# Attention over 128 graphs: the score matmuls on 32x64 tiles of the array, from keys stored once and without zero blocks

## What is computed

```python
q, k, v = heads(x @ Wq + bq), heads(x @ Wk + bk), heads(x @ Wv + bv)
scores = jnp.einsum('bhqd,bhkd->bhqk', q, k) * scale
scores = jnp.where(adj[:, None] == 0, -jnp.inf, scores)
attn = softmax(scores)
out = jnp.einsum('bhqk,bhkd->bhqd', attn, v) @ Wo + bo
return layernorm(x + out)
```

## Time and profile before

| | us |
|---|---|
| median of 3 runs | 854.3 |
| lowest, highest | 853.88, 855.64 |
| the profiled execution | 854.11 |
| its span in the trace | 852.3 |

### The profile page before, as it was taken

One profiled execution on the slowest core, in us unless ns is written; L12 is line 12 of the kernel. 1 busy time (PEld: TensorE's weight loads), 2 busy tenths in 40 slices (PEclk: granted clock), 3 DMA queues, 4 the chain that ended last, 5 costly groups with the idle time before them and its releaser, 6 DMA issues.

```text
span 852.3 us, 17597 instructions
## 1 busy us (share of the span) xinstructions
PE 834.7 (98%) x7177; PEld 688.5 (81%) x7177; DVE 540.2 (63%) x726; ACT 284.6 (33%) x401; POOL 479.7 (56%) x412
## 2 busy tenths in 40 slices
PE   8999999999999999999999999999999999999985
PEld 6878888888888888888888888888888878888863
DVE  4675557765567665567665577655577655676685
ACT  6552333332333332343332333423333423423210
POOL 3284567545566554666645575555665545654365
PEclk9999999999999999999999999999999999999998
DMA  8224343133433325333143431334333243321332
GB/s 326 70 81 138 100 142 101 53 116 100 155 99 87 103 67 155 100 109 108 64 132 100 149 97 48 129 88 155 100 88 105 72 147 100 106 76 50 112 97 90
DMA packets 50143, 91.86 MB, mean 108 GB/s; under 512 B 11280, under 2 KB 13328, under 8 KB 47888
## 3 DMA queue, kind: packets, MB, share of 16 engines
q1 hardware_dynamic: 37200, 72.91, 27.1%
q10 hardware_dynamic: 12864, 17.84, 7.5%
HBM read 40.37 MB, written 16.78 MB: 67 GB/s over the span
## 4 chain that ended last, share of the span: by engine, by line
PE 91%; DVE 4%; POOL 2%; issue 1%; ACT 1%; ACTq 1%; DMA 0%; POOLq 0%; DVEq 0%
PE ring L272 20%; PE ring L273 20%; PE ring L274 20%; PE psum_s L323 6%; PE ring L337 6%; PE ring L349 6%; PE ring L350 6%; PE ring L353 6%; ACTq L502 1%; DVE soft L599 1%; POOL qt L184 0%; POOL row L184 0%; DMA qt<-in_wq 0%; DVE top L607 0%; DVE total L611 0%
## 5 line engine op out<-in xcount | busy, mean ns | idle before, releaser
L633 DVE TENSOR_TENSOR row<-ring,row 128x512 f32<-128x512 f32 x60 | 41.5, 691 | 212.4 <-PE ring L353 212.4
L748 POOL TENSOR_TENSOR soft<-soft,top 128x1024 f32<-128x1024 f32 x62 | 118.9, 1918 | 79.6 <-DVE top L607 79.6
L177 POOL TENSOR_TENSOR soft<-soft,inverse 128x1024 f32<-128x1024 f32 x62 | 123.3, 1989 | 25.1 <-DVE inverse L614 22.1
L753 POOL TENSOR_TENSOR shifted<-moments,eps 128x1 f32<-128x1 f32 x64 | 12.1, 189 | 207.4 <-DVE moments L638 207.4
L482 ACT ACTIVATE kt<-ring,bk_slot,in_slot 128x512 f32<-128x512 f32 x128 | 92.5, 773 | 57.0 <-PE ring L274 57.0
L272 PE MATMUL ring<-wv_hi,x_hi 128*128 128x512 f32 x256 | 103.0, 402 | 0.0
L272 PE MATMUL ring<-x_hi,wq_hi 128*128 128x512 f32 x256 | 100.4, 392 | 1.1 <-DVE x_lo L649 1.1
L272 PE MATMUL ring<-x_hi,wk_hi 128*128 128x512 f32 x256 | 99.8, 390 | 0.8 <-ACT kt L482 0.8
L273 PE MATMUL ring<-x_lo,wq_hi 128*128 128x512 f32 x256 | 100.3, 392 | 0.0
L274 PE MATMUL ring<-x_hi,wq_lo 128*128 128x512 f32 x256 | 100.2, 391 | 0.0
L744 POOL TENSOR_TENSOR row<-row,bo 128x512 f32<-128x512 f32 x60 | 78.3, 1305 | 38.6 <-DMA row<-in_x 38.6
(11 more groups left out here) (77 smaller groups left out, 1485.8 us busy)
## 6 DMA issues: line engine op xcount, KB each, us to landing
pt<-soft SPq DMA_DIRECT2D x248, 64.0 KB, 2.3
pt<-soft ACTq DMA_DIRECT2D x248, 64.0 KB, 2.3
x_raw<-in_xt SPq DMA_DIRECT2D x15, 1024.0 KB, 6.5
row<-in_x SPq DMA_DIRECT2D x60, 256.0 KB, 3.2
out_rows<-row SPq DMA_DIRECT2D x60, 256.0 KB, 2.1
adj<-in_adj SPq DMA_DIRECT2D x16, 128.0 KB, 2.6
kt<-in_wk SPq DMA_DIRECT2D x4, 256.0 KB, 7.3
row<-in_wv SPq DMA_DIRECT2D x1, 1024.0 KB, 9.9
```

What stands on the lines that cost most here:

```text
L177: ops.tensor_tensor(soft_of(c), soft_of(c), on_keys(inverse[:, c % 2, :]), ALU.mult).then_inc(done, 1)
L748: nc.gpsimd.tensor_tensor(soft_of(c), soft_of(c), on_keys(top[:, c % 2, :]), ALU.subtract).then_inc(centred, 1)
```

## The change

The keys are stored once (`kt` as large as `qt`), by one ScalarE instruction with the plain bias; `in_slot` and `bk_slot` and what makes them are gone. A score matmul takes one head: 32 rows, 64 columns of weights, 64 moving columns, on a 32x64 tile of the array, of which there are eight. There are 32 for a tile of nodes instead of 16. The four row groups of the array must write to different banks, so `psum_s` is laid out by the head's place in its chunk (`HC`, four banks), and each bank now holds both tiles of a pass. For that reason `mask` waits for the scores of both tiles, `score` for the masks of both tiles of the pass before, and near the end `mix(T - 4)` for the mask of the last tile. The scores come to `soft` in another order of heads; `mix` picks them by it, with the same tiles and columns as before. The mask that GpSimd writes is repeated for the four chunks (1024 elements for each partition instead of 256).

```diff
-        kt = sb("kt", [P, 2, KC, 2 * GT, 2, NODES])
+        kt = sb("kt", [P, 2, KC, D])
...
-        bias = sb("bias", [P, 2, GT, NODES])
+        bias = sb("bias", [P, 2, GT, 2, KC, SQ])
...
-        psum_s = ctx.enter_context(nc.psum_tensor("psum_s", [P, 2, 2, D], F32))
+        psum_s = ctx.enter_context(nc.psum_tensor("psum_s", [P, HC, 2, 2, KC, SQ], F32))
...
             def score(c):
                 buf, t = c // GT % 2, c % GT
-                wait_for(pe, masked, c - 1)
+                wait_for(pe, masked, c // 2 * 2)
...
                     for graph in range(2):
-                        rows = slice(t * P + graph * NODES, t * P + (graph + 1) * NODES)
-                        for pair in range(2):
-
-                            f = slice(pair * 2 * DH, (pair + 1) * 2 * DH)
-                            last = nc.tensor.matmul(
-                                psum_s[graph * NODES:(graph + 1) * NODES, c % 2, pair,
-                                       kc * 2 * NODES:(kc + 1) * 2 * NODES],
-                                qt[f, buf, kc, rows],
-                                kt[f, buf, kc, 2 * t + graph, :, :].rearrange("p s k -> p (s k)"),
-                                start=True, stop=True)
+                        own, rows = (slice(graph * NODES, (graph + 1) * NODES),
+                                     slice(t * P + graph * NODES, t * P + (graph + 1) * NODES))
+                        for r in range(HC):
+                            f = slice(r * DH, (r + 1) * DH)
+                            last = nc.tensor.matmul(psum_s[own, r, c % 2, :, kc, :], qt[f, buf, kc, rows],
+                                                    kt[f, buf, kc, rows].rearrange("p (b k) -> p b k", k=SQ),
+                                                    start=True, stop=True)
...
-                                            pt[:, c % 2, :, r // 2 * 2 * KC + kc * 2 + r % 2, :],
+                                            pt[:, c % 2, :, r * KC + kc, :],
...
-            pe.wait_ge(masked, T - 1)
+            pe.wait_ge(masked, T)
             mix(T - 4)
-            pe.wait_ge(masked, T)
             mix(T - 3)
...
-                for s in range(2):
-                    last = nc.scalar.activation(kt[:, buf, m, :, s, :], by_graph(k_bank(J)), ACT.Identity,
-                                                bias=bk_slot[:, s, m:m + 1], scale=in_slot[:, s:s + 1])
-                last.then_inc(k_done, 1)
+                nc.scalar.activation(kt[:, buf, m, :], k_bank(J), ACT.Identity,
+                                     bias=bk[:, m:m + 1], scale=1.0).then_inc(k_done, 1)
...
-                dve.wait_ge(scored, c + 1)
+                dve.wait_ge(scored, c // 2 * 2 + 2)
...
                 nc.vector.tensor_tensor(
-                    soft_of(c),
-                    psum_s[:, c % 2].rearrange("p r (h b k) -> p (r h) b k", b=2, k=SQ)
-                    .rearrange("p h b k -> p b h k"),
-                    bias[:, c // GT % 2, c % GT, :].rearrange("p (b k) -> p b k", k=SQ).unsqueeze(2)
-                    .to_broadcast([P, 2, HEADS, SQ]),
+                    soft_of(c).rearrange("p b (r c) k -> p b r (c k)", r=HC),
+                    psum_s[:, :, c % 2].rearrange("p r b c k -> p b r (c k)"),
+                    bias[:, c // GT % 2, c % GT].rearrange("p b c k -> p b (c k)").unsqueeze(2)
+                    .to_broadcast([P, 2, HC, KC * SQ]),
                     ALU.add).then_inc(masked, 1)
...
-                nc.gpsimd.tensor_scalar(bias[:, G % 2], adj[:, :, :], 0.0, MASKED, ALU.is_equal,
-                                        ALU.mult).then_inc(bias_done, 1)
+                nc.gpsimd.tensor_scalar(
+                    bias[:, G % 2].rearrange("p t b c k -> p (t b) c k"),
+                    adj[:, :, :].rearrange("p t (b k) -> p (t b) k", k=SQ).unsqueeze(2)
+                    .to_broadcast([P, 2 * GT, KC, SQ]),
+                    0.0, MASKED, ALU.is_equal, ALU.mult).then_inc(bias_done, 1)
```

More of the change, by code:

```diff
@@ L64, in attention_kernel @@
         adj = sb("adj", [P, GT, NODES], I32)
-        bias = sb("bias", [P, 2, GT, NODES])
-        in_slot = sb("in_slot", [P, 2])
-        bk_slot = sb("bk_slot", [P, 2, KC])
+        bias = sb("bias", [P, 2, GT, 2, KC, SQ])
         bq = sb("bq", [P, KC])
@@ L96, in attention_kernel @@
         const_done, warm_done = sem("const_done"), sem("warm_done")
-        slots_done, bk_done, bias_done = sem("slots_done"), sem("bk_done"), sem("bias_done")
+        bias_done = sem("bias_done")
         x_hi_done, x_lo_done = sem("x_hi_done"), sem("x_lo_done")
@@ L110, in attention_kernel @@
         pe_went_on, dve_went_on, pool_went_on = sem("pe_went_on"), sem("dve_went_on"), sem("pool_went_on")
-        w_raw = [qt[:, 1],
-                 kt[:, 1].rearrange("p c g s k -> p (c g s k)")[:, 0:KC * D].rearrange("p (c n) -> p c n", n=D),
-                 row[:, :, :],
+        w_raw = [qt[:, 1], kt[:, 1], row[:, :, :],
                  soft[:, :, :, :, :].rearrange("p a b h k -> p (a b h k)").rearrange("p (c n) -> p c n", n=D)]
@@ L120, in at, with s_bank @@
             return ring[(p % 2 * 2 + n) % 4][:, :]
+        def s_bank(n):
+            return psum_s[:, n].rearrange("p t b c k -> p (t b c k)")
         def v_bank(c):
@@ L138, in ot_bank @@
             if 2 * FULL <= c < 2 * FULL + 2:
-                return psum_s[:, c % 2, 0, :]
+                return s_bank(c % 2 * 2)
             if c >= 2 * FULL + 2:
@@ L148, in y_bank @@
                 return ring[c % 2][:, :]
-            return psum_s[:, c % 2, 1 if c < 2 * FULL + 2 else 0, :]
+            return s_bank(c % 2 * 2 + (1 if c < 2 * FULL + 2 else 0))
         def soft_of(c):
@@ L177, in normalise @@
             ops.tensor_tensor(soft_of(c), soft_of(c), on_keys(inverse[:, c % 2, :]), ALU.mult).then_inc(done, 1)
-        def by_graph(ap):
-            return ap.rearrange("p (g k) -> p g k", k=NODES)
         def norm_row(eng, ops, c):
@@ L524, in _ @@
             act.wait_ge(qk_b_in, DMA * 2)
-            act.wait_ge(bk_done, 2)
             read_q(0)
@@ L757, in make_rstd @@
                                         ALU.pow).then_inc(row_rstd, 1)
-            for r in range(HC):
-                for s in range(2):
-                    nc.gpsimd.memset(in_slot[r * DH:(r + 1) * DH, s:s + 1],
-                                     1.0 if r % 2 == s else 0.0).then_inc(slots_done, 1)
-                    pool.wait_ge(slots_done, r * 2 + s + 1)
             nc.gpsimd.memset(eps[:, :], EPS)
@@ L767, in _ @@
             pool.wait_ge(const_done, 1)
-            pool.wait_ge(qk_b_in, DMA * 2)
-            for s in range(2):
-                nc.gpsimd.tensor_scalar(bk_slot[:, s, :], bk[:, :], in_slot[:, s:s + 1], None,
-                                        ALU.mult).then_inc(bk_done, 1)
             make_bias(0)
```

## The result

The changed kernel takes 864.6 us (median of 4 runs, 863.2 to 866.2) where the kernel before takes 854.85 (4 runs beside it, 853.9 to 855.6): a ratio of 1.0115, with a 95% interval of 1.0093 to 1.0138. The forecast of 833.6 was wrong, in sign as well, and 864.6 lies outside its range of 827 to 856. The profiled execution has a span of 864.4 us, 12.1 longer than before.

What follows compares the result with a forecast made beforehand. TensorE's stream was taken to bound the kernel: 854.1 us less 20.7 (30 score groups by 0.69) gave 833.4, and 0.2 for the median made the forecast 833.6. The range was 827 to 856, with 0.58 on 827 to 840.

Steps and rivals of the forecast that it cites:

- What bounds the kernel: Whole kernel: TensorE, busy for 98% of the span, so time taken out of its stream is time gained.
- Part 1: Score group: 128 matmuls on eight 32x64 tiles, a burst every 56 ns, 1.08 us by array work against 1.91.
- (c): Score group: the array's front allows only four matmuls at once; 0.07 us more a group, 856 us; chance 0.07.
- (d): Score group: mean spacing of 30 ns a matmul is the floor; 1.9 us more a group, 911 us; chance 0.06.
- Part 2: Feeding the score group: 3.4 ns an instruction, semaphore instructions add 0.14 us in the mean; group 1.22 us, gain 0.69.
- (a): Score group: sequencer takes 6.5 ns an instruction; group 1.77 us, 0.14 gained by 30 groups, 850 us; chance 0.14.
- (b): Score group: sequencer takes 9.7 ns an instruction; group 2.34 us, 0.43 more by 30, 867 us; chance 0.10.
- Part 3: Groups that count: 30 of 32, the last two gains turning into waits; 30 by 0.69 = 20.7 us.
- The clock: Near the end: lower granted clock after TensorE's idle time, worth up to 2 us either way, put at nothing.
- Part 4: Other engines: fewer ScalarE key reads and GpSimd's mask table (1.9 us) hidden; VectorE's mask addition left at 1.23 us.
- rival (e): VectorE's mask addition costs 2.11 us: 0.33 us new wait on ot_lo each pass, 10 us back, 843; chance 0.05.
- The added wait: First tile's mask waits for second tile's scores, done at some 412.3; VectorE reaches it at 412.81, so not late.

Runs made afterwards that it cites:

- the kernel in halves: The kernel before with each score matmul made in two halves of 64 moving columns, on its old 64x64 tiles: 871.4 us, 1.0206 of before.

## Why the prediction was wrong

**What bounds the kernel** was read rightly: TensorE's stream. So was **Part 1**, the array. The score line and its narrow windows after (columns as in the earlier trace rows):

```profile
L321 PE MATMUL psum_s<-kt,qt x4096: 211/217/266, 32.2 to 821.4; 32*64 32x64 f32 x196
...
155.05:155.12 0.07, 0.06 (x8) 0.06 (x9) 1.00 0.00 0
155.12:155.18 0.06, 0.06 (x10) 0.06 (x18) 1.00 0.00 0
155.05:155.30 0.25, 0.24 (x27) 0.24 (x33) 1.00 0.00 0
155.05:155.50 0.45, 0.44 (x39) 0.44 (x41) 1.00 0.00 0
155.05:155.90 0.85, 0.84 (x77) 0.84 (x81) 1.00 0.00 0
155.05:156.30 1.25, 1.24 (x115) 1.24 (x120) 1.00 0.00 0
155.05:156.70 1.65, 1.59 (x128) 1.46 (x128) 1.00 0.00 0
```

A matmul takes 217 ns, 52 less than in the earlier trace rows (54 expected), and in the first 0.07 us eight run, where there were four. While the sequencer's lead lasts, 27 have started in 0.25 us. By their records that is three bursts of eight, 6 or 7 ns from start to start, and the beginning of a fourth; behind the first wait for weights they stand 58 and 59 ns apart, so the step of 56 ns was near. Rivals (c) and (d) fall with it. The floor of (d), which the Trainium skill has (TensorE: Matmul & The Clock Gate, Wait — 56ns, not 53.3ns?), is broken not only inside a burst but in the mean: 1.53 us for 128 are 12 ns a start.

**Part 2, the step that was mis-sized.** From 155.50 on the starts are even, 76 in 0.80 us: 10.5 ns a matmul, 5.3 ns an instruction. I read that as the sequencer and not the array, since instructions that give the array nothing to do lengthen the group (the semaphore instructions below), while in the kernel in halves, whose array work fills 2.17 us, the same three more lengthen nothing. I had taken 3.4, by giving a semaphore instruction in the stream the 100 ns that two in a row are apart, and so taking too much off the sprint of the earlier trace rows. What such an instruction costs in the stream can be read now: groups with three more of them take 0.07 us more (548.00 to 549.60 against 522.62 to 524.14), 23 ns each. With 23 instead of 51 or 100 ns the same sprint gives (310 - 2 x 23) / 32 = 8.3 ns, so it wasn't the sequencer's own pace either; it was an upper bound, and I treated it as a difference from which the right cost would leave the right rate. The lead was longer than the 40 instructions taken (some 30 matmuls rather than 20 went out fast). So a group takes 1.53 or 1.60 us, not 1.22, in the mean 0.35 less than 1.91 and not 0.69, and 30 of them make some 10.4 us, not 20.7. Rival (a)'s rate, 6.5 ns, was the better one, and its place on the shortlist deserved more than 0.14.

**The step that is absent.** The sum counted what an instruction costs the sequencer that hands it over, and not what it costs to bring it there. That term stood at nothing without a reason, and it measured 14.2 us in 11 pauses, more than the score groups gained. The number of TensorE's instructions went up by 28%, all of it into the densest place of the program, and the page before had a line on it that I never used: the 57 pieces of its instruction queue. It also had the symptom, an issue wait of 0.7 us on the mixing line, in a place where 256 instructions go out in 3.8 us; I had looked for waits on other engines alone, and this one is on none. Rival (b) came out near in time (867 for 864.6), but for another reason: its 2.34 us group isn't there. The Trainium skill describes the pieces (Runtime: NRT & Kernel Launch, Instruction fetch mechanics: blocks of 16 KiB, 256 instructions, brought by the sequencer's own queue while the one before runs). It also says that their cost is "mostly hidden", since a sequencer gives out instructions more slowly than they come in. The trace agrees with the first (73 pieces for 18,450 instructions) and not with the second: at 3.4 us for 384 instructions, 10 pauses of 0.6 to 3.3 us on the mixing line.

**Part 3, the ends.** The gains of the last two groups are lost, as said: from the last score matmul to the last matmul it took 31.5 us before and 32.05 after. The rule that all other groups count was right as well, only there was a loss to count with them. The clock, put at nothing, cost 2.2 us behind two of the pauses. The one wait for pt (2.1 us) was not foreseen either: in the second pass TensorE is at the second mixing group some 1.0 us earlier than before, and the transfer lands 1.1 us later (53.88 against 52.81). Why it lands later was not tried.

**Part 4, the other engines.** In the groups of the changed kernel (count, busy us, mean ns, idle before and releaser):

```profile
L182 DVE TENSOR_SCALAR row<-row,moments,rstd 128x512 f32<-128x512 f32 x58 | 46.2, 797 | 20.2 <-POOL rstd L749 20.2
L475 ACT ACTIVATE kt<-ring,bk 128x512 f32<-128x512 f32 x64 | 44.0, 687 | 67.8 <-PE ring L272 67.8
L726 POOL TENSOR_SCALAR bias<-adj 128x1024 f32<-128x1024 int32 x16 | 58.4, 3649 | 13.3 <-DMA adj<-in_adj 13.3
...
L590 DVE TENSOR_TENSOR soft<-psum_s,bias 128x1024 f32<-128x1024 f32 x62 | 75.6, 1220 | 5.4 <-PE psum_s L321 4.6 <-DMA pt<-soft 0.4 <-issue 0.3
```

The keys' read is once 687 ns instead of twice 773, and hidden. The mask table takes 3.65 us, not 1.9, near the upper bound of 4.3, and is hidden all the same. One thing was not foreseen: the normalisation's last step on VectorE (L182) takes 797 ns in the mean, 518 before, so 16 us more of busy time, which is hidden too; why it is longer was not tried. The mask addition stays at 1.22 us and rival (e) falls; no wait on ot_lo stands in the middle. The added wait on both tiles' scores costs nothing that can be seen.

**The range.** Its upper end took in (a) and (c), both of them prices of the score group. The only loss outside the group that any case had was the wait on ot_lo in (e), and none had one in the supply of instructions, so the range could not hold it.

## What to carry to other kernels

Where a change splits matmuls into more and shorter ones, count TensorE's instructions (two for each matmul) in the longest row of short ones, and set them against the 256 of a piece: here rows of 256 (3.8 us) had one pause in the whole span, and rows of 384 (3.4 us) had one in every third pass. The waits view shows such a pause as "issue", in the middle of a group that has nothing to wait for, and a long one can have a stretch at the lower clock behind it. At the start of a group look first whether a transfer landed there; five such waits in these traces were named "issue" too. Break such a row with large matmuls that have to be done anyway. A stretch in which the kernel before already shows an issue wait, however short, is one without room.

## What the runs showed of the hardware

- TensorE's instructions come in pieces of 256, two pieces never less than 3.2 us apart. In a pause TensorE goes on 1.2 to 1.6 us after the piece that it lacks has been moved, and never less than 2.16 us after it has begun to move. From 3.2 us and 256 an estimate for a very long row is one instruction in some 13 ns; no row here is long enough to show it. A pause lies at fixed places in the file of instructions: behind the 4237th matmul in five kernels and the 4238th in a sixth, and at the same remainder by 256 in all. What sets the time that a piece takes stays open; no run varied the size of a piece.
- Out of what is at hand, TensorE's sequencer hands over an instruction in 5.3 ns, a matmul with its weights in 10.5; a semaphore instruction among matmuls costs 23 ns, not its recorded 51. Why it is 5.3 and not less was not tried.
- Eight 32x64 tiles of the array work at once on 64 columns each, with a burst of eight starts every 58 or 59 ns, as long as instructions are at hand (the first three bursts of a group).
- The order of the work has a price of its own: project_v between scores and mixing costs the kernel before 7.7 us (0.26 in each pass), where moving the mixing ahead costs nothing (854.9 for 854.0). With the pauses gone the narrow tiles are worth it, but only just: 851.2 us against 853.55 in the runs beside it.
